# Second graph layer: window sums that begin at the lowest receiver and go to a table in node order

## The chip, the cores and the metric

One core of one Trainium2 chip. The metric is the device time of one launch in microseconds (us). A span is the time from the first to the last instruction of one profiled execution.

## What is computed

A graph of 3125 nodes with 256 features each and 50000 edges, sorted by receiver (`dst`). Two layers follow each other, each with a residual sum and a layer norm:

```
x = layernorm(x + L0(x, edge_attr, src, dst))     # mean over each sender of an MLP times a gate
x = layernorm(x + L1(x, src, dst, w))
```

The change concerns `L1`, attention with four heads of 64 columns:

```
h     = x @ W                                # [nodes, 4 heads, 64]
e     = leaky(a_src[src] + a_dst[dst]) * w   # per edge and head
e_exp = exp(e - max(e))
denom = segment_sum(e_exp, dst)
alpha = e_exp / (denom[dst] + 1e-10)
out   = segment_sum(h[src] * alpha, dst)
```

## The kernel before

The edges are cut into 391 blocks of 128, four blocks to a group (98 groups), two groups to a pair (49 pairs). There are 25 node tiles of 128 rows. All five instruction streams are written out by hand, with semaphores.

**First layer, to about 1610 us.** The matrix engine is busy nearly all the time with the MLP; nothing of it is changed, but for the table that is cleared during it (`HB`, at groups 8 to 10) and two small instructions of constants at the start (`rem_c`).

**Between the layers, to about 1670 us.** The first norm, the products `h` with the score columns, and their table `HT` in DRAM. Ahead of it VectorE works out constants (`win_tile`, `keep`, `in_tile` and a test on the graph, `outside`) while the last additions to the first layer's table land.

**Windows, about 1671 to 2334 us.** GpSimd fetches the sender rows of each block with one indirect DMA (`gather_h_rows`, L1605) into a ring of 12 groups; group g may be fetched when VectorE has weighted group g - 12 (`s_xb`). For each pair q VectorE does, in this order: `weighted_rows(2q)`, `carry_window(2q-2)`, `running_maximum(q+1)`, `edge_scores(q+2)` (it waits for the gathers of pair q+2 and for the product of TensorE that gives the receivers' scores), `weighted_rows(2q+1)`, `carry_window(2q-1)`, `one_hot(q+3)`, `window_rows(q+1)`. Every seventh pair `window_scores` is put in, and once, at q = 3, `last_rows`: eleven instructions (L1153 to L1164), some of 2450 elements per partition, which find for each node the last window that holds it. TensorE sums a group's blocks into one PSUM bank (`window_sums`, L1927): the row of a sum is the receiver modulo 128 (`in_window`). Since the edges are sorted, consecutive groups overlap, and `carry_window` (L1136, L1148) adds to a window the window before, row by row where `keep` says that the row still means the same node, times `drop`, the correction for a raised maximum:

```
dve.scalar_tensor_tensor(hist[:, g % HISTR, 0:BW], hist[:, (g - 1) % HISTR, 0:BW], carried,
                         PS[g % 3][:, 0:BW], ALU.mult, ALU.add).then_inc(s_carry, 1)
```

SP stores each window as 128 rows of the table `HB` (L1485), six of them in flight (`s_hd[g % HISTR]`). ScalarE only takes the exponentials (L2178, L2185, L2187).

**End, from about 2334 us.** VectorE makes `scale` from `last_g` and the factors of the windows (L1192, L1194). When all windows are stored GpSimd fetches, with 25 indirect DMAs (L1671), each node's last window row into `fin`. The tiles go in chunks of 3, 5, 5, 5, 5 and 2. `attention_residual` on VectorE: four small instructions for the denominators (L1298 to L1305), a product of the rows with them into PSUM (`weigh`, L1117), the sum with `xn` (L1321), statistics (L962, L966); `norm_factors` (L994, L996). ScalarE normalises (L2153), SP stores `out` (L1533).

`if_outside` is a branch for graphs on which windows do not suffice. It is not taken here; each engine loads a register and jumps.

Of the kernel before, what the change touches and what calls it, by code (L numbers as in the profile page):

```python
# [6 lines left out]
P = 128  # L7
# [15 lines left out]
def build_program(nc, xT, x, src_cols, dst_cols, src_row, dst_row, eT, w_cols,  # L23
# [50 lines left out]
    ZERO_ROW = NG * P  # L74
    ACC0 = ZERO_ROW + P
    HROWS = ACC0 + TR
# [73 lines left out]
    with ctx:  # L150
# [15 lines left out]
        HB = nc.dram_tensor("HB", [HROWS, BW], f32).ap()  # L166
# [13 lines left out]
        rem_c = sb("rem_c", [P, NB])  # L180
# [22 lines left out]
        zeros = sb("zeros", [P, BW])  # L203
# [36 lines left out]
        rem_ci = sb("rem_ci", [P, NB], i32, sn)  # L240
# [59 lines left out]
        keep = sb("keep", [P, NG], f32, sc)  # L300
# [4 lines left out]
        reached = sb("reached", [P, NT, NG], bf16, sc)  # L305
        in_tile = sb("in_tile", [P, NG, NT], bf16, sc)
        n_f = sb("n_f", [P, NT], f32, sc)
        base_f = sb("base_f", [P, 1], f32, sc)
        passed = sb("passed", [P, NT], f32, sc)
        there = sb("there", [P, NT], f32, sc)  # L310
        row_f = sb("row_f", [P, NT], f32, sc)
        row_i = sb("row_i", [P, NT], i32, sc)
        node = sb("node", [P, NT, HEADS], f32, sc)
        ADC = 14
        picked = sb("picked", [P, ADC, HEADS, NT], f32, sc)
        ad_w = sb("ad_w", [P, NG, HEADS], f32, sc)
# [6 lines left out]
        drop_k = sb("drop_k", [P, NQ], f32, sc)  # L323
        last_g = sb("last_g", [P, NT, NG], bf16, sc)
        factor = sb("factor", [P, NG], f32, sc)
        chosen = sb("chosen", [P, NT, NG], f32, sc)
        scale = sb("scale", [P, NT], f32, sc)
# [19 lines left out]
        hist = sb("hist", [P, HISTR, BW], f32, s2)  # L347
# [10 lines left out]
        trash_u = sb("trash_u", [P, 1], f32, s2)  # L358
# [141 lines left out]
        s_dk = sem("s_dk")  # L500
        s_carry = sem("s_carry")
        s_hd = [sem(f"s_hd{i}") for i in range(HISTR)]
# [20 lines left out]
        VW = C1 + 2 * C2 + 5  # L523
# [22 lines left out]

        assert NG % 2 == 0 and NG % ADC == 0 and ADC % 2 == 0 and HGR > 6 and HGR % 2 == 0
# [67 lines left out]
        def wait_windows_stored(eng):  # L615
            for k in range(HISTR):
                eng.wait_ge(s_hd[k], ring_total(HISTR, k, NG))
# [13 lines left out]
        def _(dve):  # L631
# [116 lines left out]
            for p in range(4, 2 * NT):  # L748
# [23 lines left out]
                if p == 42:  # L772
# [3 lines left out]
                    const(dve.tensor_single_scalar(rem_ci[:, :], dst_c[:, :], P - 1, ALU.bitwise_and))  # L776
# [354 lines left out]
            def carry_window(g):  # L1131
# [6 lines left out]
                if g >= HISTR:  # L1138
                    dve.wait_ge(s_hd[g % HISTR], 16 * (g // HISTR))
# [27 lines left out]
            for q in range(-3, NQ + 1):  # L1167
# [19 lines left out]
                if q == ADC // 4:  # L1187
                    last_rows()
# [1091 lines left out]
```

## Time and profile before

| | |
|---|---|
| median of 3 runs | 2392.39 us (2390.41 to 2396.98) |
| the profiled execution | 2400.63 us, span 2398.6 us |
| mean granted TensorE clock | 0.892 of full speed |
| TensorE matmul, VectorE, ScalarE, GpSimd busy | 1909.3, 1425.6, 1208.7, 1519.2 us |
| first layer | 0 to about 1610 us |
| windows of the second layer | about 1671 to 2334 us |
| end | about 2334 us to 2398.6 us |

The busy shares are means over stages that have different limits, so the windows and the end are read by themselves. In the rows "remote" and "another core or an unknown queue" stand for a releaser that the profile could not name.

### The profile page before, as it was taken

What the parts mean: (1) busy time and instruction counts of PE and PEld (TensorE: products, weight loads), DVE (VectorE), ACT (ScalarE), POOL (GpSimd) and SP (SyncE); (2) the same over time, 40 slices, a digit from 0 to 9 for tenths busy, and PEclk for the clock granted to TensorE, in tenths of its full rate; (3) what the DMA queues carried; (4) which work ended last, traced back from release to release, by engine and by line L of the source; (5) the groups of instructions that cost most, each with busy time, mean ns of one, the idle gap of its engine ahead of it and who ended that gap; (6) DMA issues with size and microseconds to landing.
All of it is one profiled execution on the core that took longest, in us unless ns stands there. A gap on an engine that the chain in (4) does not pass through costs nothing. (4 is left out here: it accounts for less than half of the span.)

```text
span 2398.6 us, 38205 instructions
## 1 busy us (share of the span) xinstructions
PE 1909.3 (80%) x12132; PEld 1633.2 (68%) x12132; DVE 1425.6 (59%) x4037; ACT 1208.7 (50%) x2298; POOL 1519.2 (63%) x1253
## 2 busy tenths in 40 slices
PE   7799999989999999999999999966145555555560
PEld 6688888878888888888888888855033444444440
DVE  6556666556666666666666666646164554554575
ACT  2477677666777777777777777744000000000012
POOL 0417677777777777777777777752745655655623
PEclk9899999999999999999999999988567777667785
DMA  7788877777777777777777877766434544444433
GB/s 245 254 224 185 176 164 165 142 150 171 163 159 161 160 160 161 166 158 159 159 161 167 176 171 173 162 107 194 113 94 118 128 118 128 128 117 129 127 82 110
DMA packets 239708, 370.94 MB, mean 155 GB/s; under 512 B 33256, under 2 KB 172482, under 8 KB 239496
## 3 DMA queue, kind: packets, MB, share of 16 engines
q0 software_dynamic: 104688, 191.38, 40.0%
q1 hardware_dynamic: 134807, 177.00, 25.9%
q8 instruction: 101, 1.65, 0.3%
q14 instruction: 112, 0.91, 0.1%
HBM read 260.28 MB, written 107.97 MB: 154 GB/s over the span
## 5 line engine op out<-in xcount | busy, mean ns | idle before, releaser
L1548 POOL DMA_INDIRECT accA<-ystage,to_a x391 | 642.4, 1643 | 217.0 <-issue 113.3
L1554 POOL DMA_INDIRECT GA<-TA,src_c x391 | 429.7, 1099 | 252.3 <-issue 111.8
L1605 POOL DMA_INDIRECT Hg<-HT,src_c x391 | 375.0, 959 | 255.7 <-DVE xb L1117 147.5
L643 DVE TENSOR_TENSOR h2l<-h2f,h2h 128x512 fp32r<-128x512 f32 (+1 forms) x294 | 203.0, 690 | 314.1 <-ACT h2h L1998 160.1
L1680 PE MATMUL bank<-h1h,W1h 128*128 128x512 f32 x882 | 354.7, 402 | 11.0 <-DVE h1l L643 11.0
L2035 ACT ACTIVATE h1f<-bank 128x512 f32<-128x512 f32 (+1 forms) x392 | 221.0, 590 | 256.9 <-PE bank L1735 196.8
L1682 PE MATMUL bank<-h1h,W1l 128*128 128x512 f32 x882 | 349.1, 396 | 0.0
L1681 PE MATMUL bank<-h1l,W1h 128*128 128x512 f32 x882 | 349.0, 396 | 0.0
L2178 ACT ACTIVATE drop<-neg_m 128x1 f32<-128x1 f32 x49 | 14.4, 295 | 603.6 <-issue 418.3
L1927 PE MATMUL bank<-xb,in_window 128*128 128x260 f32 (+1 forms) x782 | 279.7, 518 | 47.6 <-issue 47.2
L643 DVE TENSOR_TENSOR h1l<-h1f,h1h 128x512 fp32r<-128x512 f32 x294 | 194.3, 688 | 117.8 <-ACT h1h L1998 107.5
L2060 ACT ACTIVATE h2f<-bank,b1c 128x512 f32<-128x512 f32 x294 | 201.9, 687 | 120.4 <-PE bank L1752 95.9
L1927 PEld LDWEIGHTS bank<-xb,in_window 128*128 128x128 f32 (+1 forms) x782 | 194.4, 262 | 96.1 <-issue 59.3
L1916 PE MATMUL bank<-diag,ones 128*128 128x128 f32 x98 | 34.2, 448 | 275.2 <-issue 162.1
L1916 PEld LDWEIGHTS bank<-diag,ones 128*128 128x128 f32 x98 | 23.4, 286 | 293.2 <-issue 172.4
L1680 PE MATMUL bank<-W2h,h2h 128*128 128x256 f32 (+1 forms) x782 | 220.7, 282 | 2.1 <-DVE ystage L809 2.1
L1681 PE MATMUL bank<-W2l,h2h 128*128 128x256 f32 (+1 forms) x782 | 221.0, 283 | 0.0
L1682 PE MATMUL bank<-W2h,h2l 128*128 128x256 f32 (+1 forms) x782 | 221.0, 283 | 0.0
L1680 PEld LDWEIGHTS bank<-h1h,W1h 128*128 128x128 f32 x882 | 167.5, 190 | 42.7 <-DVE h1l L643 11.8
L1682 PEld LDWEIGHTS bank<-h1h,W1l 128*128 128x128 f32 x882 | 166.9, 189 | 39.6
L1681 PEld LDWEIGHTS bank<-h1l,W1h 128*128 128x128 f32 x882 | 167.2, 190 | 37.1
L1998 ACT ACTIVATE h2h<-h2f 128x512 fp32r<-128x512 f32 x294 | 185.4, 631 | 9.4
(252 smaller groups left out, 4490.6 us busy)
## 6 DMA issues: line engine op xcount, KB each, us to landing
ef<-in_eT SPq DMA_DIRECT2D x97, 256.0 KB
bcast_i<-in_src_row SPq DMA_DIRECT2D x97, 256.0 KB
TW<-TB SPq DMA_DIRECT2D x116, 203.0 KB
HB<-hist SPq DMA_DIRECT2D x98, 130.0 KB
rel<-RL SPq DMA_DIRECT2D x97, 128.0 KB
rem<-RD SPq DMA_DIRECT2D x48, 256.0 KB
TB<-stB SPq DMA_DIRECT2D x24, 406.0 KB
accA<-zeros SPq DMA_DIRECT2D x4, 2193.0 KB, 16.4
```

The costliest lines, as they stand in the source:

```text
L643: return dve.tensor_tensor(o, full, hi.bitcast(f32), ALU.subtract)
L1548: return pool.indirect_dma_start(out=table, out_offset=bass.IndirectOffsetOnAxis(ap=rows, axis=0), in_=sums, in_offset=None, compute_op=AL ...
L1554: pool.indirect_dma_start(out=GA[0:n, b % (GAR * BLOCKS_PER_GROUP), :].bitcast(f32), out_offset=None, in_=TA, in_offset=bass.IndirectOffse ...
L1605: pool.indirect_dma_start(out=Hg[0:n, slot, :], out_offset=None, in_=HT, in_offset=bass.IndirectOffsetOnAxis(ap=src_c[0:n, b:b + 1], axis= ...
L1680: pe.matmul(o, lh, rh, start=first, stop=False)
L1681: pe.matmul(o, lh, rl, start=False, stop=False)
L1682: return pe.matmul(o, ll, rh, start=False, stop=last)
L1916: pe.matmul(PTOP[:, 0:P], ones[:, :], diag[:, q % 2, :], start=True, stop=True).then_inc(s_sp, 1)
L1927: last = pe.matmul(PS[g % 3][:, 0:BW], in_window[0:n, j, :], xb[0:n, j, :], start=b == blocks[0], stop=b == blocks[-1])
L1998: return act.activation(o, i, ACT.Copy)
L2035: act.activation(h1f[0:k1(c), c, 0:n], PT[u % 2][0:k1(c), 0:n], ACT.Tanh).then_inc(s_tanh1, 1)
L2060: act.activation(h2f[:, m, 0:n], PL1[u % 2][:, 0:n], ACT.Tanh, bias=b1c[:, m:m + 1]).then_inc(s_tanh2, 1)
```

## The change

1. **Windows begin at the lowest receiver.** `in_window` compares with `rel_c` (receiver less the group's lowest receiver) in place of `rem_c` (receiver modulo 128). A window is then 128 consecutive nodes.
2. **The sum before is carried by a matmul.** VectorE no longer adds in `carry_window`. It builds `to_next`, a unit matrix shifted by the distance between the two windows' first nodes, for even groups times `drop`; TensorE adds `to_next` times the stored window before as a fifth matmul of the group; ScalarE copies the sum out of PSUM (`window_copy`), and a 261st column with the negative maximum of that window.
3. **Stores go to a table in node order.** SP reads the group's lowest receiver into a register and stores the window at that row of `F`. Successive windows overlap there, so each store waits for the one before (one semaphore `s_hd`). `last_rows`, `keep`, `drop_k`, `factor`, `chosen` and `scale` go; a plain load of the 261st column (`row_m`) and one exponential take the place of `scale`.
4. **End.** SP loads `row_m` and the six chunks of `fin` with plain DMAs in place of the 25 gathers. VectorE makes the reciprocal with two instructions; GpSimd multiplies the rows by it in place; VectorE adds and takes the statistics as before.

```diff
-            def carry_window(g):
...
-                dve.scalar_tensor_tensor(hist[:, g % HISTR, 0:BW], hist[:, (g - 1) % HISTR, 0:BW], carried,
-                                         PS[g % 3][:, 0:BW], ALU.mult, ALU.add).then_inc(s_carry, 1)
+            def carry_matrix(g):
...
+                if g >= 3:
+                    dve.wait_ge(s_S, g - 1)
+                o, shifted = to_next[:, g % 2, :], moved[:, g:g + 1]
+                if g % 2:
+                    dve.tensor_scalar(o, iota_p, shifted, None, ALU.is_equal).then_inc(s_next, 1)
+                    return
+                dve.wait_ge(s_drop, g // 2 + 1)
+                dve.tensor_scalar(o, iota_p, shifted, drop[:, g // 2:g // 2 + 1], ALU.is_equal, ALU.mult).then_inc(s_next, 1)
...
-                if q == ADC // 4:
-                    last_rows()
...
 def window_sums(g):   # TensorE
+                if g >= 1:
+                    pe.wait_ge(s_next, g)
+                    pe.wait_ge(s_carry, g)
+                    last = pe.matmul(PS[g % 3][:, 0:BW], to_next[:, g % 2, :], hist[:, (g - 1) % HISTR, 0:BW],
+                                     start=False, stop=True)
...
 # ScalarE
+            def window_copy(g):
+                act.wait_ge(s_S, g + 1)
+                if g >= HISTR:
+                    act.wait_ge(s_hd, 16 * (g - HISTR + 1))
+                copy(hist[:, g % HISTR, 0:BW], PS[g % 3][:, 0:BW])
+                copy(hist[:, g % HISTR, BW:FW], neg_m[:, g // 2 + 1:g // 2 + 2]).then_inc(s_carry, 1)
             for q in range(NQ):
+                if q >= 2:
+                    window_copy(2 * q - 4)
+                    window_copy(2 * q - 3)
...
 # SP
-                        sp.wait_ge(s_carry, g + 1)
-                        sp.dma_start(HB[g * P:(g + 1) * P, :], hist[:, g % HISTR, :]).then_inc(s_hd[g % HISTR], 16)
+                        first = sp.value_load(low_i[0:1, g:g + 1], min_val=0, max_val=N - 1)
+                        sp.wait_ge(s_carry, g + 1)
...
+                            sp.wait_ge(s_hd, 16 * g)
+                        sp.dma_start(F[bass.ds(first, P), :], hist[:, g % HISTR, :]).then_inc(s_hd, 16)
...
+            wait_windows_stored(sp)
+            sp.dma_start(row_m[:, :], F[0:NT * P, BW:FW].rearrange("(t p) d -> p (t d)", p=P),
+                         allow_slow_non_contiguous=True).then_inc(s_rowm, 16)
+            for c in range(NC):
+                tiles = tiles_of_chunk(c)
+                sp.dma_start(fin[:, tiles[0]:tiles[-1] + 1, :],
+                             F[tiles[0] * P:(tiles[-1] + 1) * P, 0:BW].rearrange("(t p) d -> p t d", p=P)).then_inc(s_fin[c], 16)
...
 # GpSimd
-            for t in range(NT):
-                pool.indirect_dma_start(
-                    out=fin[:, t, :], out_offset=None, in_=HB,
...
+            for c in range(NC):
+                pool.wait_ge(s_cinv, NC + c + 1)
+                pool.tensor_tensor(rows, rows, cinv[:, v, :].unsqueeze(3).to_broadcast([P, k, HEADS, HD]), ALU.mult)\
+                    .then_inc(s_att, 1)
...
 # VectorE, end
+            attention_factors(0)
+            for c in range(NC):
+                if c + 1 < NC:
+                    attention_factors(c + 1)
                 if c >= 1:
                     norm_factors(c - 1, NC + c - 1)
+                attention_residual(c)
```

On VectorE, in the middle of the windows, one pair read before (`L1117` is the weighting, `L1079` to `L1101` the scores, `L1148` the carried sum):

```order
L1117 TENSOR_TENSOR xb<-Hg,bank 128x4x256
L1136 TENSOR_TENSOR drop_k<-drop,keep 128x1
L1148 SCALAR_TENSOR_TENSOR hist<-hist,drop_k,bank 128x260
L1108 TENSOR_REDUCE top_g<-bank 128x1
L1112 SCALAR_TENSOR_TENSOR neg_m<-top_g,neg_m 128x1
L1079 TENSOR_TENSOR score<-Hg,bank 128x32
```

and reads now:

```order
L1110 TENSOR_TENSOR xb<-Hg,bank 128x4x256
L1136 TENSOR_SCALAR to_next<-bank,moved,drop 128x128
L1101 TENSOR_REDUCE top_g<-bank 128x1
L1105 SCALAR_TENSOR_TENSOR neg_m<-top_g,neg_m 128x1
L1072 TENSOR_TENSOR score<-Hg,bank 128x32
```

Between the wait for a pair's scores and the weighting behind it nothing is moved.

On TensorE, in the middle of the windows, one pair now reads as follows (`L1898` are the block sums, `L1903` the carried window, `L1878` the receivers' scores, `L1887` the spread of the maxima):

```order
L1887 MATMUL bank<-diag,ones 128x128
L1898 MATMUL bank<-xb,in_window 128x260 x4
L1903 MATMUL bank<-hist,to_next 128x260
L1878 MATMUL bank<-ad_p,hot 128x4 x24
L1898 MATMUL bank<-xb,in_window 128x260 x4
L1903 MATMUL bank<-hist,to_next 128x260
```

The two `L1903` rows are new; the first of them, with its wait for ScalarE, stands ahead of the product for the receivers' scores.

## Rows read from the trace of the kernel before

**Rows 1.** Busy time by stretch (us, then PE, PEld, DVE, ACT, POOL; clock, DMA share, GB/s)

```profile
150.00:1550.00 1400.00, 1369.42 (x8952) 1199.26 (x8951) 893.93 (x2724) 1027.65 (x1855) 1050.68 (x760) 0.99 0.78 166
1900.00:2100.00 200.00, 107.70 (x648) 81.52 (x645) 100.16 (x222) 11.61 (x48) 118.57 (x125) 0.75 0.48 125
```

**Rows 2.** Waits, 1900 to 2100 us (total us, times, longest)

```profile
DVE score L1079 <- remote: 88.3, 13, 9.8
POOL Hg L1605 <- DVE xb L1117: 48.1, 15, 5.0
```

**Rows 3.** Timeline, 1960 to 1991 us (start us, us, instruction, idle before it)

```profile
1960.93 0.75 PE L1907 MATMUL bank<-ad_p,hot 128*128 128x4 bf16 x24
...
1972.79 0.19 DVE L1079 TENSOR_TENSOR score<-Hg,bank 128x32 f32<-128x32 f32 x1 [9.82 <-remote]
...
1978.81 0.82 PE L1907 MATMUL bank<-ad_p,hot 128*128 128x4 bf16 x24
...
1984.18 0.96 POOL L1605 DMA_INDIRECT Hg<-HT,src_c  x1 [0.30 <-issue]
1985.44 0.19 DVE L1079 TENSOR_TENSOR score<-Hg,bank 128x32 f32<-128x32 f32 x1 [6.10 <-remote]
...
1986.54 1.22 DVE L1117 TENSOR_TENSOR xb<-Hg,bank 128x1024 f32<-128x1024 f32 x1
1988.02 0.95 POOL L1605 DMA_INDIRECT Hg<-HT,src_c  x1 [2.89 <-DVE xb L1117]
```

**Rows 4.** Timeline around `last_rows`, VectorE and GpSimd

```profile
1788.21 0.29 DVE L1153 TENSOR_SCALAR n_f<-tile_row,p_f 128x25 f32<-128x25 f32 x1
...
1789.55 2.71 POOL L1605 DMA_INDIRECT Hg<-HT,src_c  x1 [0.30 <-issue]
...
1797.08 1.22 DVE L1117 TENSOR_TENSOR xb<-Hg,bank 128x1024 f32<-128x1024 f32 x1
...
1798.57 0.95 POOL L1605 DMA_INDIRECT Hg<-HT,src_c  x1 [5.05 <-DVE xb L1117]
```

**Rows 5.** Groups by line: VectorE 1750 to 2250 us, TensorE 1900 to 2100 us

```profile
L1148 DVE SCALAR_TENSOR_TENSOR hist<-hist,drop_k,bank 128x260 f32<-128x260 f32 x38 | 18.4, 485 | 8.2 <-DVE drop_k L1136 6.5 <-issue 1.5
...
L1101 DVE TENSOR_SCALAR diag<-ident,top_c 128x128 f32<-128x128 f32 x38 | 12.2, 322 | 1.8 <-issue 0.2 <-DVE top_c L1096 0.2
...
L1136 DVE TENSOR_TENSOR drop_k<-drop,keep 128x1 f32<-128x1 f32 x38 | 5.7, 151 | 0.0
L1927 PE MATMUL bank<-xb,in_window 128*128 128x260 f32 x248 | 90.5, 527 | 11.6 <-issue 11.6
```

**Rows 6.** ScalarE's copies between the layers (ns min/median/max)

```profile
L1998 ACT ACTIVATE hst<-bank x25: 371/390/391, 1633.2 to 1668.2; 128x264 f32<-128x264 f32 x24, 53x264 f32<-53x264 f32 x1
```

**Rows 7.** Timeline of the last pairs of windows and of the first gather behind them

```profile
2306.89 0.16 DVE L1112 SCALAR_TENSOR_TENSOR neg_m<-top_g,neg_m 128x1 f32<-128x1 f32 x1
...
2313.37 0.16 DVE L1112 SCALAR_TENSOR_TENSOR neg_m<-top_g,neg_m 128x1 f32<-128x1 f32 x1
...
2333.38 0.48 DVE L1148 SCALAR_TENSOR_TENSOR hist<-hist,keep,bank 128x260 f32<-128x260 f32 x1 [0.61 <-PE bank L1927]
...
2342.66 0.96 POOL L1671 DMA_INDIRECT fin<-HB,row_i  x1 [43.12 <-issue]
...
2348.21 0.17 DVE L1298 TENSOR_TENSOR cden<-fin,scale 128x12 f32<-128x12 f32 x1 [8.99 <-DMA fin<-HB,row_i]
```

**Rows 8.** Chain that ended last, DMA piece behind the last window

```profile
2333.89 4.46 DMA HB<-hist
```

**Rows 9.** Timeline, SP's loads of single elements (64 of 4 bytes each) and of rows

```profile
319.59 0.60 SPq L1450 DMA_DIRECT2D ablk<-in_a_src x1
```

**Rows 10.** DMA issues of the whole span (KB each, us to landing)

```profile
tab<-accA SPq DMA_DIRECT2D x8, 645.0 KB, 8.0
```

**Rows 11.** Timeline of the end on VectorE

```profile
2366.09 0.42 DVE L962 BATCH_NORM_STATS2 stats<-xn 128x6 f32<-128x256 f32 x1
...
2375.57 0.18 DVE L966 BATCH_NORM_AGGREGATE mv<-stats 128x2 f32<-128x6 f32 x1 [0.52 <-remote]
...
2384.14 0.18 DVE L1300 TENSOR_SCALAR cden<-cden 128x20 f32<-128x20 f32 x1
...
2384.88 1.62 DVE L1117 TENSOR_TENSOR bank<-fin,bank 128x512 f32<-128x512 f32 x3
...
2386.71 1.74 DVE L1321 TENSOR_TENSOR xn<-xn,bank 128x256 f32<-128x256 f32 x5
2388.37 1.72 DVE L962 BATCH_NORM_STATS2 stats<-xn 128x6 f32<-128x256 f32 x5
2390.01 0.43 DVE L966 BATCH_NORM_AGGREGATE mv<-stats 128x2 f32<-128x6 f32 x5
...
2390.52 0.17 DVE L1300 TENSOR_SCALAR cden<-cden 128x8 f32<-128x8 f32 x1
...
2393.40 0.28 DVE L966 BATCH_NORM_AGGREGATE mv<-stats 128x2 f32<-128x6 f32 x2
```

**Rows 12.** Timeline between the layers, VectorE and GpSimd side by side

```profile
1645.46 1.47 DVE L974 TENSOR_TENSOR tab<-tab 128x1290 f32<-128x1290 f32 x1
...
1647.34 0.19 POOL L1613 COPY node<-hst 128x4 f32<-128x4 f32 x1 [0.25 <-ACT hst L1998]
```

**Rows 13.** All GpSimd copies of that line (ns min/median/max)

```profile
L1613 POOL COPY node<-hst x25: 179/187/1162, 1633.8 to 1668.6; 128x4 f32<-128x4 f32 x24, 53x4 f32<-53x4 f32 x1
```

More of the change, by code:

```diff
@@ L322, in build_program @@
         drop = sb("drop", [P, NQ], f32, sc)
[L323 to L327, printed above, removed]
+        row_m = sb("row_m", [P, NT], f32, sc)
+        row_eps = sb("row_eps", [P, NT], f32, sc)
+        log_eps = sb("log_eps", [P, 1], f32, sc)
         Wc = sb("Wc", [P, DK, OUT + 2 * HEADS], f32, sc)
@@ L499, in build_program @@
         s_S = sem("s_S")
-        s_dk = sem("s_dk")
+        s_next = sem("s_next")
         s_carry = sem("s_carry")
-        s_hd = [sem(f"s_hd{i}") for i in range(HISTR)]
+        s_hd = sem("s_hd")
+        s_rowm = sem("s_rowm")
         s_nd = sem("s_nd")
@@ L615, in wait_windows_stored @@
         def wait_windows_stored(eng):
-            for k in range(HISTR):
-                eng.wait_ge(s_hd[k], ring_total(HISTR, k, NG))
+            eng.wait_ge(s_hd, 16 * NG)
         def if_outside(eng):
@@ L1166, in _ @@
+                if g >= 3:
[6 more added lines that the diff above has]
+                dve.tensor_scalar(o, iota_p, shifted, drop[:, g // 2:g // 2 + 1], ALU.is_equal, ALU.mult).then_inc(s_next, 1)
             window_scores(0)
-            for q in range(-3, NQ + 1):
+            for q in range(-3, NQ):
@@ L1285, in _ @@
                                                   ALU.is_equal, ALU.mult))
-                    step(dve.tensor_scalar(to_u[0:n, :], to_f[0:n, 1:2], trash_u[0:n, :], None, ALU.add), ("row", b))
+                    step(dve.tensor_scalar(to_u[0:n, :], to_f[0:n, 1:2], trash[0:n, :], None, ALU.add), ("row", b))
                     dve.wait_ge(s_vg, 64 * NB + 16 * (b + 1))
@@ L1311, in attention_residual @@
-                for j in range(0, k, 2):
-                    m = min(2, k - j)
-                    last = weigh(bank[3 * (c % 2) + j // 2][:, 0:m * OUT].rearrange("p (t d) -> p t d", d=OUT),
-                                 fin[:, t0 + j:t0 + j + m, 0:OUT], factors[:, j:j + m], P, m)
-                last.then_inc(s_att, 1)
+                dve.wait_ge(s_att, c + 1)
+                for t in tiles:
+                    n = rows_of_tile(t)
+                    dve.tensor_tensor(xn[0:n, t, :], xn[0:n, t, :], fin[0:n, t, 0:OUT], ALU.add).then_inc(s_res, 1)
@@ L1322, in attention_residual @@
-                row_stats(tiles, NT)
-            for c in range(NC):
                 attention_residual(c)
@@ L2189, in _ @@
                 last.then_inc(s_ex, 1)
-            for i in range(2):
-                last = act.activation(factor[:, :].rearrange("p (q i) -> p q i", i=2)[:, :, i], neg_m[:, 1:NQ + 1], ACT.Exp,
-                                      bias=neg_m[:, NQ:NQ + 1], scale=-1.0)
-            last.then_inc(s_factor, 1)
+            for g in range(NG - 4, NG):
+                window_copy(g)
             with if_outside(act):
```

140 lines of the change are left out of this document (51 added, 89 removed).

## Prediction

> **What bounds the kernel now.** I first read the busy time by stretch. In the first layer TensorE is busy 1369 of 1400 us, and nothing of the change lies there. In the windows no engine is full: of 200 us TensorE is busy 107.7, VectorE 100.2, GpSimd 118.6, ScalarE 11.6 [rows 1]. So I read the waits next. VectorE loses 88.3 us in 13 waits at the scores (L1079), with no releaser named, and GpSimd loses 48.1 us in 15 waits for VectorE's weighted rows [rows 2]. The timeline of one pair shows how the two hang together. GpSimd's last fetch starts at 1984.18, the score wait ends at 1985.44, the odd group is weighted at 1986.54 for 1.22 us, and only then, at 1988.02, does GpSimd fetch again after 2.89 us of idle time [rows 3]. Eight fetches of 0.96 + 0.30 us are 10.1 us; with the stall of 2.5 to 2.9 a pair takes about 12.6 us. It is a closed loop: ring empty, scores, weighting, ring free. What VectorE does *outside* the 2.5 us between score wait and weighting is hidden in its 6.10 us of waiting [rows 3]. The reader should keep this in mind: the change works nearly only on that outside part.
>
> At the end the fetches of `fin`, VectorE's chunks and the store follow one another. The last window is summed at 2333.38, stored after 4.46 us more, the first denominator starts at 2348.21, and a full chunk takes 6.38 us (2384.14 to 2390.52) [rows 7, 8, 11].
>
> **The change part by part.**
>
> *Steady windows: 0.* Per pair VectorE loses two additions of 0.485 and one product of 0.151, and gains two `to_next` of 128x128, for which the nearest row is `diag`, 0.322 [rows 5]. That is 0.48 us less per pair, in time in which VectorE waits. TensorE gains two products of 260 columns, 2 x 0.527 at the most, on 107.7 us busy in 200 [rows 1, 5]; ScalarE two copies of about 0.39, the price of a copy of 264 columns out of PSUM [rows 6], and two of one column. Cover for both: TensorE ends the receivers' product (L1907, 24 matmuls) at 1961.7 and at 1979.6, while the score waits on it end at 1972.79 and 1985.44, so 11 and 6 us later, and each just as GpSimd has run out of fetches [rows 3]. Stores wait for each other, but two of 4.46 us at the most fit into 12.6 [rows 8]; without that cover six stored windows of slack would be used up first. If TensorE's cover is gone, the second rival holds.
>
> *`last_rows`: -6.6.* It holds VectorE from 1788.21 to 1797.08, 8.87 us, once. The weighting behind it is what GpSimd waits for: it idles 5.05 us, and one fetch beside it takes 2.71 us in place of 0.95 [rows 4]. 5.05 + 1.76 = 6.8, of which I take 6.6, for the part of the stall that every pair has is partly in it. Bounds: 0, if the next gathers absorb it, to 8.9.
>
> *Last pairs: -2.* After the last fetch VectorE sets the pace, 6.48 us per pair (2306.89 to 2313.37) [rows 7]. 0.48 less work and up to 0.2 less waiting in some five pairs give 2 to 4; TensorE with its two more products is nearly as long, so I take 2.
>
> *Last window to first factor: +2.5.* Before it is 2348.21 - 2333.86 = 14.35 us: store 4.46, then GpSimd's start at 2342.66, then the fetch [rows 7, 8]. Now: one more product 0.44 to 0.53, copies 0.39 + 0.25, a store of 4.46 or less, then `row_m`, then the first chunk of `fin`. `row_m` is a load of 3200 single elements of 4 bytes. The one row on such a load issues 64 of them in 0.60 us [rows 9]; scaled to 3200 that is 30 us, and if elements are spread over the queue's engines it is a few: bounds 2 and 30, and I take 8, for the issue row holds a fixed part and is paid once. The first `fin` chunk lies behind it: a load of 645 KB took 8.0 us to land, this one is 400 KB, of which I count 3 beyond `row_m`, since they overlap [rows 10]. 0.5 + 0.6 + 3.9 + 8 + 3 + 0.9 (exponential and reciprocal) = 16.9, against 14.35: +2.5. With the bounds of `row_m` the step is -4 to +25.
> The Trainium skill (DMA: Bandwidth & Descriptors, section Rules for kernel authors) says that a strided last dimension turns into one descriptor per element and names it as a thing to avoid; by that rule this load is nearer to the 30 than to the 2, and the step would be about +24 in place of +2.5. No row here shows a load of this size.
>
> *Chunks of the end: -6.4.* From the first denominator to the end the span now takes 2398.6 - 2348.21 = 50.4 us [rows 7]. VectorE alone then does, per chunk of five tiles, factors 0.45, sums 1.74, statistics 1.72, aggregates 0.43 and norms 0.35: 4.7 us [rows 11]. The product of 1.62 goes to GpSimd as one instruction of 1280 elements in SBUF. No row shows such a product there. GpSimd's copy of 4 columns takes 0.187, as VectorE's small ones take 0.17 [rows 11, 13], so parity, 1.62, is my lower bound; four times that, 6.4, the upper; I take twice, 3.2, nearer to the copy than to the far end.
> With both engines side by side a chunk is VectorE's 4.7 to 4.9. But rows show them in each other's way: GpSimd's copy takes up to 1.162 where VectorE's two-input additions of 1.47 run [rows 12, 13], and a fetch of 0.95 took 2.71 beside `last_rows` [rows 4]. The order on VectorE is factors of chunk c+1, norms of c-1, sums of c. So GpSimd's product of c+1 starts just ahead of norms and sums, which have two SBUF inputs. If the two exclude each other, VectorE stands for the whole 3.2, and then works 4.7 less the factors' end: 7.7 a chunk, above the 6.38 of now. Against this, 10 us go: from 2366.09 to 2375.57 VectorE's statistics and aggregates come one by one with 0.5 to 1.2 us between, 9.7 us for 2.1 of work, while GpSimd still issues fetches [rows 11]; with no fetches of GpSimd left that stretch has no ground. The sum is 5 x 7.7 = 38.5, and 5.5 behind the last aggregate (2393.40 to 2398.6 is 5.2): 44 us, -6.4. Bounds: five chunks of 4.9 and some 7 for the start and the last normalisation, 31.5 (-19); with GpSimd at 6.4 and exclusion, 16 more than my 44 less what the statistics cover, so +6 to +13.
> The Trainium skill (SBUF — State Buffer, section SBUF: two separate sides) says that GpSimd and VectorE share a port under an exclusive lock, which a VectorE operation with two SBUF inputs holds against GpSimd. By that rule the trace agrees: 1.162 in place of 0.187. [...]
>
> *Sum:* -6.6 - 2 + 2.5 - 6.4 = -12.5. The profiled execution took 2400.6 us, 8.2 above the median of 2392.4; 2392.4 - 12.5 = 2380.
>
> **Rivals.**
> 1. *Engines run side by side at the end.* No exclusion, GpSimd at 2 us or so: the end is 31.5, so the sum is about -25 and the time 2367. For it: GpSimd's copies are short in the median [rows 13].  Against: the longest of them.
> 2. *A new loop through ScalarE (slower).* Place: the product L1903 waits for ScalarE's copy of the window before, and the receivers' scores stand behind it on TensorE. TensorE's window sums, 248 of 90.5 us in 200 [rows 5], 5.8 us a pair, become a chain sum, copy, sum. It decides when the score wait ends on the receivers' product and not on the fetches. Price: a carry of 0.44 with 0.64 of copies and signals of 0.3, 1.45 us a pair, times 48 is 70 us: 2450 at full price, about 2415 at half. For it: the score wait has no named releaser, and ScalarE is in order behind exponentials that wait for the same scores. Against: TensorE had finished 6 to 11 us ahead [rows 3].
> 3. *The single-element load or GpSimd's product is slow.* `row_m` at 20 us or more, or products at 6.4: +12 to +22 on my sum, so 2392 to 2402, 2395 in the middle.
> 4. *The change does nothing.* `last_rows` absorbed (0 in place of -6.6) and the end a wash: 2390, no difference.
>
> **How the numbers follow.** The forecast has 0.45, with a range of its own of 2370 to 2390; rival 1 has 0.2, rival 2 0.17, rival 3 0.13, rival 4 0.05. A measurement tells 0.3% (7.2 us) from nothing, so faster is below 2385.2 and slower above 2399.6. Faster: 0.4 of the forecast and 0.2 of the first rival = 0.6. Slower: all of rival 2 and a good third of rival 3, 0.22. The rest, 0.18, is within 0.3%. The range leaves out the far part of rival 1 and most of rival 2: 2362 to 2404.
>
> **What would show it.** Right: the period of a pair in the middle stays at 12.6 us, the wait at the scores stays about 6 us; the stall at 1798 is gone; the chunk on VectorE is 6 to 7.7 us with GpSimd's product at 3 us and longer beside the sum; the first factor is 16 to 18 us behind the last sum. Wrong: L1903 with long idle time behind ScalarE, the score wait ending on TensorE, a `row_m` of tens of us, or GpSimd's product above 6 us with VectorE idle before each sum.

## The result and the profile after

| | before | changed | ratio (95% interval) |
|---|---|---|---|
| the runs shown | 2390.51 us (2386.91 to 2400.23, 20 runs) | 2399.14 us (2391.30 to 2405.38, 20 runs) | 1.0032 (1.0021 to 1.0043) |
| beside it in e13 | 2384.55 us (29 runs) | 2390.90 us (12 runs) | 1.0032 (1.0011 to 1.0053) |
| beside it in e5, on a chip where before takes 2219 us | 2218.60 us (29 runs) | 2212.76 us (12 runs) | 0.9974 (0.9961 to 0.9988) |

Forecast was 2380 us, 0.4% to 0.5% faster. Measured was 0.3% slower, at the edge of what a measurement tells from nothing, and twice the same. On a chip where the kernel before runs 170 us faster the sign turns round. That third row became the key to the case. Launches in a second, slower state are left out of all ratios: one of the kernel before beside e1 to e4 (2462.49 us) and two of e18 (2712.53 and 5719.66 us).

The profiled execution of the changed kernel took 2397.9 us (span 2396.1). It lies near its median, while the one of before lay 10 us above its own. So stages are compared here by their own lengths, and where possible with a second profile of each. From the first fetch of the windows to the last start of a matmul in them:

| stage | before (profile; e16) | changed (profile; e13) |
|---|---|---|
| windows | 661.9; 649.8 us | 682.8; 672.9 us |
| last matmul to first denominator | 15.3; 14.3 us | 10.6; 11.1 us |
| first denominator to the end | 50.4; 49.7 us | 38.6; 38.3 us |

e16 is the kernel before with `last_rows` moved, 2383.61 us in the median. The end gave back 3 to 5 and 12 us; the windows took 21 to 23. Taken crosswise the four profiles give 11 to 33 us for the windows, so the 20 us are good to some 10.

The waits of the windows, 1900 to 2100 us, changed kernel (total us, times, longest), beside [rows 2]:

```profile
DVE score L1072 <- remote: 106.6, 13, 11.1
ACT hist L1974 <- remote: 87.8, 14, 10.0
ACT hist L1974 <- PE bank L1903: 73.4, 12, 6.6
...
POOL Hg L1576 <- DVE xb L1110: 54.4, 15, 5.2
```

VectorE's wait for the scores grew from 88.3 to 106.6 us and GpSimd's stall from 48.1 to 54.4. The busy time in the same stretch (us, PE, PEld, DVE, ACT, POOL) shows the same, 117 fetches where there were 125 [rows 1], one pair's worth or 6% less:

```profile
1900.00:2100.00 200.00, 120.37 (x681) 91.92 (x682) 94.54 (x207) 23.07 (x103) 114.77 (x117) 0.74 0.44 117
```

The granted TensorE clock of the stretch is 0.74 against 0.75 [rows 1] and explains nothing of it (e13 0.76 and e16 0.73, the other way round).

Now a pair in the timeline of the changed kernel, to be read beside [rows 3]:

```profile
1959.39 0.74 PE L1878 MATMUL bank<-ad_p,hot 128*128 128x4 bf16 x24
...
1967.04 0.95 POOL L1576 DMA_INDIRECT Hg<-HT,src_c  x1 [0.30 <-issue]
1970.64 0.19 DVE L1072 TENSOR_TENSOR score<-Hg,bank 128x32 f32<-128x32 f32 x1 [11.12 <-remote]
1970.65 0.39 ACT L1974 ACTIVATE hist<-bank 128x260 f32<-128x260 f32 x1 [7.71 <-remote]
...
1973.06 3.81 PE L1898 MATMUL bank<-xb,in_window 128*128 128x260 f32 x8 [0.38 <-issue]
...
1973.23 1.21 POOL L1576 DMA_INDIRECT Hg<-HT,src_c  x1 [5.24 <-DVE xb L1110]
...
1976.65 0.77 PE L1903 MATMUL bank<-hist,to_next 128*128 128x260 f32 x2
...
1977.26 0.75 PE L1878 MATMUL bank<-ad_p,hot 128*128 128x4 bf16 x24
1977.46 0.39 ACT L1974 ACTIVATE hist<-bank 128x260 f32<-128x260 f32 x1 [6.33 <-PE bank L1903]
```

Three things. L1878's records end at 1960.13, and both VectorE and ScalarE, which wait for two different signals of TensorE, start at 1970.64 and 1970.65. ScalarE's product had ended at 1966.53. Two engines released within 0.01 us, 10 and 4 us behind the work that they wait for, suggest that the release and not the work came late. The whole trace bears this out: in 23 of the 42 middle pairs (scores 4 to 45) the two start within 0.02 us of each other. But not every signal is late. ScalarE starts 0.04 us behind the end of L1903 in 35 of its 67 waits from 1800 to 2250 us (the last row above is one, amid fetches without a break), and about 4 us behind it in most of the others; on the chip of the third row (e5) it is 0.04 in 75 of 75. Second, L1878 now starts behind L1903, 0.6 us after it. L1903 does not wait for ScalarE's copy there: it starts at 1976.65, while the block sums, which last to 1976.87, are still in the records, and so it does in all 46 odd groups of this profile and of e13's. Third, the first fetch behind the stall takes 1.21 us where it took 0.95.

The end on VectorE, GpSimd and ScalarE, one chunk, beside [rows 11]:

```profile
2371.34 2.33 POOL L1643 TENSOR_TENSOR fin<-fin,cinv 128x1280 f32<-128x1280 f32 x1 [4.13 <-DVE cinv L1265]
2371.47 2.21 DVE L984 SCALAR_TENSOR_TENSOR shift<-mv,rstd 128x5 f32<-128x5 f32 x1
2373.61 1.75 DVE L1273 TENSOR_TENSOR xn<-xn,fin 128x256 f32<-128x256 f32 x5
...
2375.29 1.72 DVE L950 BATCH_NORM_STATS2 stats<-xn 128x6 f32<-128x256 f32 x5
2376.93 0.42 DVE L954 BATCH_NORM_AGGREGATE mv<-stats 128x2 f32<-128x6 f32 x5
...
2377.81 2.33 POOL L1643 TENSOR_TENSOR fin<-fin,cinv 128x1280 f32<-128x1280 f32 x1 [4.14 <-DVE cinv L1265]
```

A chunk takes 2377.81 - 2371.34 = 6.47 us. GpSimd's product is 2.33 us. VectorE's five-column `shift`, 0.17 us by itself, lasts 2.21 us beside it and ends where the product ends. Its statistics, one SBUF input each, take 1.72 us as ever.

Between the last window and the first denominator:

```profile
2347.39 0.39 ACT L1974 ACTIVATE hist<-bank 128x260 f32<-128x260 f32 x1 [1.28 <-PE bank L1903]
...
2352.30 0.42 SPq L1494 DMA_DIRECT2D row_m<-F  x1
...
2356.08 0.32 ACT L2227 ACTIVATE row_eps<-row_m,log_eps 128x25 f32<-128x25 f32 x1 [8.22 <-DMA row_m<-F]
...
2357.52 0.17 DVE L1262 SCALAR_TENSOR_TENSOR cden<-row_eps,fin 128x12 f32<-128x12 f32 x1 [10.04 <-DMA fin<-F]
```

The load of 3200 single elements is issued in 0.42 us and its exponential starts 3.4 us behind that.

### The profile page after: what moved, and what is told of

The parts are those of the page before. It is cut to its first block, busy times and chain, and to the rows that moved or that the text cites. A ratio compares the mean times of both kernels' runs of the same rounds, so it can differ in the third digit from the quotient of the medians.

```text
span 2396.1 us, 39366 instructions
## 1 busy us (share of the span) xinstructions
PE 1955.6 (82%) x12326; PEld 1674.4 (70%) x12326; DVE 1394.1 (58%) x3947; ACT 1249.8 (52%) x2493; POOL 1516.4 (63%) x1234
## 4 chain that ended last, share of the span: by engine, by line
PE 57%; another core or an unknown queue 15%; DVE 13%; issue 5%; DMA 4%; ACT 2%; SPq 2%; POOL 1%; DVEq 0%; ACTq 0%; POOLq 0%
PE bank L1651 13%; PE bank L1653 13%; PE bank L1652 13%; PE bank L1706 4%; PE bank L1696 4%; DVE xb L1110 3%; PE bank L1723 3%; DVE in_window L1057 2%; PE bank L1748 2%; PE bank L1747 2%; DMA accA<-ystage,to_a 1%; PE bank L1854 1%; PE bank L1898 1%; DVE hot L1048 1%
## 5 line engine op out<-in xcount | busy, mean ns | idle before, releaser
L1525 POOL DMA_INDIRECT GA<-TA,src_c x391 | 437.7, 1119 | 252.5 <-issue 109.4
L1576 POOL DMA_INDIRECT Hg<-HT,src_c x391 | 381.7, 976 | 271.0 <-DVE xb L1110 163.0
L1974 ACT ACTIVATE hist<-bank 128x260 f32<-128x260 f32 x98 | 38.0, 388 | 530.4 <-remote 257.6
L1898 PE MATMUL bank<-xb,in_window 128*128 128x260 f32 (+1 forms) x782 | 272.2, 508 | 29.9 <-issue 29.3
L1887 PE MATMUL bank<-diag,ones 128*128 128x128 f32 x98 | 35.0, 457 | 258.3 <-DVE diag L1094 184.4
L1898 PEld LDWEIGHTS bank<-xb,in_window 128*128 128x128 f32 (+1 forms) x782 | 187.9, 252 | 75.8 <-issue 41.5
L1072 DVE TENSOR_TENSOR score<-Hg,bank 128x32 f32<-128x32 f32 (+2 forms) x50 | 9.3, 187 | 358.3 <-remote 348.0
L1887 PEld LDWEIGHTS bank<-diag,ones 128*128 128x128 f32 x98 | 23.7, 290 | 276.1 <-DVE diag L1094 198.3
L1651 PEld LDWEIGHTS bank<-h1h,W1h 128*128 128x128 f32 x882 | 167.5, 190 | 45.9 <-DVE h1l L633 10.6
```

Source lines behind the costliest of these rows:

```text
L1525: pool.indirect_dma_start(out=GA[0:n, b % (GAR * BLOCKS_PER_GROUP), :].bitcast(f32), out_offset=None, in_=TA, in_offset=bass.IndirectOffse ...
L1576: pool.indirect_dma_start(out=Hg[0:n, slot, :], out_offset=None, in_=HT, in_offset=bass.IndirectOffsetOnAxis(ap=src_c[0:n, b:b + 1], axis= ...
L1651: pe.matmul(o, lh, rh, start=first, stop=False)
L1898: last = pe.matmul(PS[g % 3][:, 0:BW], in_window[0:n, j, :], xb[0:n, j, :], start=b == blocks[0], stop=g == 0 and b == blocks[-1])
```

## The experiments

The first eight ran on a chip where the kernel before takes 2219 us, as did e17 and e18; e9 to e16 on chips where it takes 2384 us. The kernel before is timed beside each.

**e1 to e4: parts of the window stage, one at a time.** Edits against the changed kernel:

```diff
 # e1, SP
-                        first = sp.value_load(low_i[0:1, g:g + 1], min_val=0, max_val=N - 1)
-                        sp.dma_start(F[bass.ds(first, P), :], hist[:, g % HISTR, :]).then_inc(s_hd, 16)
+                        sp.dma_start(F[31 * g:31 * g + P, :], hist[:, g % HISTR, :]).then_inc(s_hd, 16)
 # e2: window_copy on VectorE (dve.tensor_copy), none on ScalarE
                 if q >= 1:
+                    window_copy(2 * q - 1)      # ahead of running_maximum and edge_scores
...
                     weighted_rows(2 * q + 1)
+                    window_copy(2 * q)
 # e3 (and e15): the order on VectorE
-                one_hot(q + 3)
                 window_rows(q + 1)
+                one_hot(q + 3)
 # e4: window_sums without
-                    last = pe.matmul(PS[g % 3][:, 0:BW], to_next[:, g % 2, :], hist[:, (g - 1) % HISTR, 0:BW],
-                                     start=False, stop=True)
```

> The changed kernel, but SP stores each window at a fixed row (31 times the group) and reads no register for it; the table is then not in node order, so the output is not the reference's. In the changed kernel the windows (first fetch to last window sum) take 683 us, before 663 us. Theory A (the 20 us come from the carried product's chain TensorE, ScalarE, TensorE in the windows): nothing moves, 681 to 685 us. Rival B (SP's reads of low_i and the moving address are the cost): about 665 us and a time near 2380.

> The changed kernel with the window copies on VectorE (one ahead of the wait for the scores, one behind the odd group's weighting) in place of ScalarE. Theory A1 (the copy stands in ScalarE's order ahead of the exponentials and holds them and the next carry): windows 665 to 675 us instead of 683. Rival A2 (TensorE's signals come late whoever waits for them): no gain, 683 us or more, since VectorE then has 1.1 us more per pair of its own and waits for the window's sum ahead of the scores: up to 700 us.

> The changed kernel with VectorE's one_hot (L1048) behind window_rows (L1057) in place of ahead of it. The first fetch behind each stall takes 1.21 us in the changed kernel and 0.95 before: it starts 0.1 us after L1048 there and 0.05 us ahead of it before. Theory C (L1048 keeps GpSimd's fetch waiting when it starts first): every first fetch takes 0.95 again, the windows lose 0.26 us in some 33 pairs, 683 - 9 = 674 us. Rival (the stretch has another ground): 1.21 stays, 683 us.

> The changed kernel without the product L1903: TensorE sums the four blocks alone, ScalarE copies and SP stores as in the change, VectorE still makes to_next. It leaves out the sum over groups of a receiver. Theory A (product and its wait for ScalarE's copy are the cost of the score wait ending 1.55 us in place of 0.26 us behind the last fetch): the score wait ends 0.3 us behind the last fetch again and the windows take 683 - 12 = 671 us (with the fetch stretch of 0.26 a pair left). Rival B (ScalarE's copies, SP's register reads or the stores): still 683 us.

| | time | before beside it | ratio (interval) | windows |
|---|---|---|---|---|
| e1 | 2213.47 us | 2219.19 us | 0.9964 (0.9945 to 0.9982) | 510.1 us |
| e2 | 2214.94 us | 2219.19 us | 0.9974 (0.9955 to 0.9993) | 509.6 us |
| e3 | 2213.87 us | 2219.19 us | 0.9973 (0.9956 to 0.9991) | 508.0 us |
| e4 | 2212.04 us | 2219.19 us | 0.9973 (0.9954 to 0.9992) | 507.3 us |

None of the expectations was met, and none could tell anything apart: the windows take 507 to 510 us here, not 683, whatever is left out. (e1 and e4 do not compute the reference's output: e1 stores at the wrong rows, e4 leaves out the sum over groups.) The waits of e4, 1800 to 2000 us, tell why:

```profile
DVE score L1072 <- DMA Hg<-HT,src_c: 69.3, 18, 4.9
POOL Hg L1576 <- issue: 48.2, 158, 0.3
POOL Hg L1576 <- DVE xb L1110: 0.3, 1, 0.3
```

The score wait ends on the rows that the fetches bring, and GpSimd never runs dry (0.3 us of stall in 200): it issues all the time, 159 fetches in 200 us, 8 x 1.257 = 10.06 us a pair. With that, 838 matmuls in a stretch of 200 us in place of 916 (e4 against e5, 1900 to 2100 us) are worth nothing.

**e5 to e8: the changed kernel itself there, the end, `last_rows`.** e5 is the changed kernel; e8 is e3 and e6 together.

```diff
 # e6, VectorE, end, the loop over chunks
-                if c + 1 < NC:
-                    attention_factors(c + 1)
-                if c >= 1:
-                    norm_factors(c - 1, NC + c - 1)
-                attention_residual(c)
+                dve.wait_ge(s_att, c + 1)
+                attention_residual(c)           # the sums alone
+                if c >= 1:
+                    norm_factors(c - 1, NC + c - 1)
+                if c + 1 < NC:
+                    attention_factors(c + 1)
+                row_stats(tiles_of_chunk(c), NT)
 # e7 (and e16), the kernel before
+            last_rows()
             window_scores(0)
...
-                if q == ADC // 4:
-                    last_rows()
```

> The changed kernel once more, as it is, beside the kernel before on the same chip. In the first four experiments the kernel before took 2219 us and not 2390, and the windows ran at 10.1 us a pair in all four, which is GpSimd's issue alone (8 x 1.257). Theory L (the loss in the windows exists only where the loop ring empty, score wait, weighting is what sets the pair: 12.6 us; where GpSimd never runs dry it is hidden): if the kernel before is near 2219 us again, the changed one is 5 to 12 us faster; if it is near 2390 us, the changed one is 4 to 12 us slower. Rival (the loss is there at either speed): slower by 0.3% both times.

> The changed kernel with another order on VectorE in the end: sums of chunk c, norms of c-1, factors of c+1, then the statistics of c. So GpSimd's product of c+1 runs beside the statistics, which read one SBUF input. Theory X (product and VectorE's operations with two SBUF inputs exclude each other: L984 takes 2.21 us beside the product, 0.17 alone): chunks go from 6.46 to 4.7 or 4.9 us, the end is 6 to 9 us shorter. Rival (VectorE waits for something else there): 6.4 us a chunk.

> The kernel before with last_rows moved ahead of the first window scores, where VectorE waits. It prices that term of the prediction (6.6 us, bounds 0 to 8.9). At 12.6 us a pair (kernel before near 2390 us): 4 to 7 us faster. Where GpSimd sets the pair at 10.1 us: the one stretched fetch only, 1 to 2 us, or if last_rows still empties the ring 5 us.

> The changed kernel with one_hot behind window_rows and with the end's other order: the version that may beat both. Near 2219 us for before: 14 to 20 us faster than before. Near 2390 us: the gain of the end (6 to 9 us) and of the fetches (9 us) on the changed kernel's 2399: 2382 to 2386.

| | time | ratio to before, 2218.60 us (interval) | windows | end |
|---|---|---|---|---|
| e5 | 2212.76 us | 0.9974 (0.9961 to 0.9988) | 507.7 us | 38.3 us |
| e6 | 2207.43 us | 0.9956 (0.9942 to 0.9970) | 507.7 us | 32.9 us |
| e7 | 2217.64 us | 1.0005 (0.9991 to 1.0019) | 512.1 us | 40.5 us |
| e8 | 2209.51 us | 0.9960 (0.9939 to 0.9981) | 507.3 us | 32.9 us |

Theory L held: where GpSimd sets the pair the changed kernel is 5.8 us faster, and its windows are no longer than those of before with `last_rows` moved (507.7 against 512.1). The loss of 20 us is there only where the ring runs dry. e7 was expected 1 to 2 or 5 us faster and shows no difference. e8 is a miss: 14 to 20 us were expected and 9 measured, no more than e6 gives alone.

e6 settles the exclusion. The timeline of its end:

```profile
2183.36 1.67 DVE L950 BATCH_NORM_STATS2 stats<-xn 128x6 f32<-128x256 f32 x5
2183.52 2.33 POOL L1642 TENSOR_TENSOR fin<-fin,cinv 128x1280 f32<-128x1280 f32 x1 [2.56 <-DVE cinv L1265]
...
2185.89 1.77 DVE L1271 TENSOR_TENSOR xn<-xn,fin 128x256 f32<-128x256 f32 x5 [0.52 <-POOL fin L1642]
2187.57 0.18 DVE L982 RECIPROCAL rstd<-std 128x5 f32<-128x5 f32 x1
2187.79 0.17 DVE L984 SCALAR_TENSOR_TENSOR shift<-mv,rstd 128x5 f32<-128x5 f32 x1
```

GpSimd's product is as long as before, 2.33 us, the statistics run beside it undisturbed, and `shift` is back at 0.17. Sums start at 2180.99 and at 2185.89, 4.9 us a chunk. The end lost 5.4 us, and the time 5.3, a little under the 6 to 9 expected.

The end is also where the chips differ once more: that of the kernel before takes 40.5 us here (e7) and 50.4 in its profile. Most of the 10 us are the stretch of [rows 11] in which VectorE's short operations came one by one; it isn't there in e7, although GpSimd fetches there too. Fetches alone are then not its ground.

**e9 to e12: the order on TensorE, and a signal made late.** Where before takes 2384 us, all four on one chip.

```diff
 # e9 (and e12, e14, e17), TensorE: L1878 between the blocks and the carried product of the odd group
-                    window_sums(2 * q + 1)
-                if q + 3 < NQ:
-                    destination_scores(q + 3)
+                    window_sums(2 * q + 1, behind)   # blocks, destination_scores(q + 3), carried product
 # e10 (before), e11 (changed), e12 (e9): the receivers' scores are signalled by SP
-                dve.wait_ge(s_ad, q + 1)
+                dve.wait_ge(s_late, 32 * (q + 1))
...
+                    sp.wait_ge(s_ad, q + 4)
+                    for i in range(2):
+                        if 2 * (q + 3) + i > 0:
+                            sp.wait_ge(s_late, 16 * (2 * (q + 3) + i))
+                        sp.dma_start(late_t[:, :], x[0:1, 0:1]).then_inc(s_late, 16)
```

> The changed kernel with the receivers' product L1878 on TensorE ahead of the odd group's carried product L1903. In the recorded profile at 12.6 us a pair the stretch from one score wait's end to the end of L1878 grew from 6.83 us to 7.4 to 7.7, and the signal behind it came after 5.1 to 6.5 us (5.77 before). Where before takes near 2390 us: theory A3 (what stands ahead of L1878 sets the pair) gives 0.4 us less per pair, 2399 - 16 = 2383; rival A4 (the late signal alone) 2399. Where before takes near 2219 us both say: as the changed kernel there, 2213.

> The kernel before, but VectorE's score wait takes TensorE's signal over two tiny loads of SP, one after the other (some 4 us later than the signal itself); the six store semaphores are three. It imitates the late signal of the recorded profile. Where the windows ran at 10.1 us a pair: L1907's end to the score goes from 3 to about 4.4 us, the loop becomes 6.8 + 4.4 = 11.2 us, the windows 510 + 45 = 555 us and the time 2265. If the signal's lateness is not what sets the pair, it stays at 2219.

> The changed kernel with the same late signal. Theory A3: with the loop in force the changed kernel's 7.4 to 7.7 us ahead of the signal count, 0.6 to 0.9 us more a pair than the kernel before with the late signal: windows 25 to 40 us longer than in e10, less the 10 us that the end and last_rows give back: 15 to 30 us slower than e10. Rival (the changed kernel loses nothing by the loop, but by signals that come later on that chip): 6 to 10 us faster than e10.

> The changed kernel with L1878 ahead of the odd group's L1903 and the late signal. Theory A3: 0.4 us less a pair than e11, so 15 to 20 us faster than e11. Rival: as e11.

| | time | ratio to before, 2383.63 us (interval) | windows |
|---|---|---|---|
| e9 | 2371.02 us | 0.9947 (0.9931 to 0.9964) | 652.8 us |
| e10 | 2485.92 us | 1.0425 (1.0403 to 1.0447) | 756.5 us |
| e11 | 2441.08 us | 1.0236 (1.0219 to 1.0254) | 730.1 us |
| e12 | 2401.42 us | 1.0069 (1.0050 to 1.0088) | 683.5 us |

e9 moves one product of 24 small matmuls ahead of another, takes no work away, and turns 0.3% slower into 0.5% faster. Its windows are 20 to 30 us shorter than the changed kernel's (652.8 against 672.9 and 682.8), and as long as those of the kernel before (661.9 and 649.8), though both carried products are still in it. Its waits, 1900 to 2100 us, against 106.6 us in 13 before the edit:

```profile
DVE score L1072 <- remote: 59.6, 11, 10.8
```

The gain is not a regular loop with one product less in it. Its pairs mostly alternate between 8 to 11 and 14 to 18 us, and L1878's 24 matmuls no longer run in one go:

```profile
1974.05 0.49 PE L1878 MATMUL bank<-ad_p,hot 128*128 128x4 bf16 x14
1975.39 0.16 PE L1878 MATMUL bank<-ad_p,hot 128*128 128x4 bf16 x1 [0.84 <-issue]
1976.80 0.21 PE L1878 MATMUL bank<-ad_p,hot 128*128 128x4 bf16 x2 [1.25 <-issue]
1977.52 0.16 PE L1878 MATMUL bank<-ad_p,hot 128*128 128x4 bf16 x1 [0.52 <-issue]
...
1984.59 0.16 PE L1878 MATMUL bank<-ad_p,hot 128*128 128x4 bf16 x1 [1.25 <-issue]
```

The last matmuls come singly, mostly 0.7 us or a multiple of it apart, with no wait in between that the profile shows, and the score follows at 1987.06. VectorE's short operations in the stretch of [rows 11] are spaced alike (2367.88, 2369.28, 2370.68, 2372.08, 2372.79). So on these chips it is not only signals that come late: at times instructions start late for which the profile shows no wait.

e10 to e12 were meant to make the loop on the other chip. They met a chip where before takes 2384 us, so the delay came on top. It cost 102 us, some 2 us a pair: about half of the 4 us that two loads were expected to take. From the end of the receivers' product to the score it is 8.7 us in the median of the middle pairs, where the profile of before has 5.8. e12 against e11 has the sign of theory A3 and twice the size, 40 us where 15 to 20 were expected. e11 against e10 is a miss: 45 us faster, where 15 to 30 slower was expected. In e10 the score wait ends on SP's tiny loads:

```profile
DVE score L1081 <- DMA late_t<-in_x: 100.3, 11, 12.1
```

They stand in one queue with the other loads and stores of SP, which the two kernels place differently, so the added delay is not the same in both. The pair e10 and e11 settles nothing; e11 and e12 differ by the order on TensorE alone.

**e13 to e16: beside each other on a further chip, where before takes 2384.55 us.** e13 is the changed kernel, e14 is e9, e3 and e6 together, e15 is e3, e16 is e7.

> The changed kernel as it is. Where before takes 2384 to 2391 us: windows 683 us and 0.3% slower than before, so e9's 12.6 us of gain over before are 20 us and more of gain over this (theory A3: the order of L1878 and L1903). Rival: near 2375, then e9's order was worth nothing. Where before takes near 2219: 2213 again.

> The changed kernel with L1878 ahead of the odd group's L1903, one_hot behind window_rows, and the end's other order (factors of the next chunk ahead of the statistics). Where before takes 2384 to 2391: e9's 13 us and the end's 5.5 us, with the fetches' 0.26 us a pair up to 9 more: 18 to 27 us faster than before. Near 2219: as e8, 9 to 10 us faster.

> The changed kernel with one_hot behind window_rows, as e3, where the first fetch lasted 0.95 to 0.98 in either order since GpSimd never ran dry. Where before takes 2384 to 2391: theory C has the first fetch behind each stall at 0.95 in place of 1.21 us and 8 to 12 us less than e13; rival (the loop has slack there, or the later one-hot matrix holds L1878 back by 1.2 us a pair): no gain, or up to 50 us slower.

> The kernel before with last_rows ahead of the first window scores. Where before takes 2384 to 2391: 2 to 7 us faster (my term was 6.6). Near 2219: no difference, as e7.

| | time | ratio to before (interval) | windows | end |
|---|---|---|---|---|
| e13 | 2390.90 us | 1.0032 (1.0011 to 1.0053) | 672.9 us | 38.3 us |
| e14 | 2371.21 us | 0.9951 (0.9932 to 0.9970) | 654.5 us | 32.9 us |
| e15 | 2397.20 us | 1.0044 (1.0024 to 1.0064) | 676.3 us | 38.3 us |
| e16 | 2383.61 us | 0.9992 (0.9977 to 1.0006) | 649.8 us | 49.7 us |

e13 repeats the result, so e9's 0.9947 stands against 1.0032, each against before on its own chip: the order is worth some 20 us. On one chip e14 is 19.7 us faster than e13; less the 5.4 us of the end's order that leaves 14. So 14 to 20 us. e15 refutes theory C as a cause: the fetch behind the stall is 0.95 us again,

```profile
1999.10 0.95 POOL L1576 DMA_INDIRECT Hg<-HT,src_c  x1 [2.73 <-DVE xb L1110]
```

and the time is no better (the intervals of e13 and e15 overlap). Where the 0.26 us a pair went was not seen. e16 prices `last_rows`: -0.9 us, by its interval between -5.5 and +1.4. e14, with that useless third edit, is a miss: 13.3 us faster than before where 18 to 27 had been expected, hardly more than e9 without the end's order.

**e17 and e18.** These met the chip of 2219 us again (before 2220.78 us). e17 is e9 and e6 without e3's edit.

```diff
 # e18, the kernel before, GpSimd, behind the four fetches of a group
+                pool.memset(pause[:, g:g + 1], 0.0)
```

> The changed kernel with L1878 ahead of the odd group's L1903 and the end's other order. Where before takes 2384 to 2391: e9's 12.6 and the end's 5.5 us, 16 to 20 us faster than before, ratio 0.992 to 0.994. Near 2219: 9 to 11 us faster (as e6), ratio 0.995 to 0.996.

> The kernel before with a memset of one element on GpSimd behind the four fetches of each group. Theory S (TensorE's signal is held while GpSimd issues fetches in one go): the score wait ends some us earlier, GpSimd never runs dry and the windows fall from 650 towards 530 us. Rival: nothing moves but the memsets, 0.2 to 0.5 us each, 98 of them: windows 0 to 45 us longer. Near 2219 for before only the second can show.

e17 took 2209.43 us, ratio 0.9946 (0.9927 to 0.9964): 11 us faster than before, as expected. e18 took 2221.93 us, ratio 0.9998 (0.9980 to 1.0017), windows 512.5 us: the short instruction costs nothing there. Theory S was not tested, since the ring does not run dry on that chip.

## Why the prediction was wrong

**Steady windows, 0: this step failed.** It took the 6 and 11 us between the end of L1907's records and the end of the score wait [rows 3] as cover, room in which TensorE may work longer. There was none: what stands ahead of that product counts, although TensorE is idle half the time. The stretch from one score start to the end of the next L1907 is score, diag, block sums, L1907; the change put the carried product of the odd group into it. In the median of the middle pairs it grew from 6.83 us to 7.57 (7.70 in e13), and in e9, with the product behind L1878 again, it is 6.84 and the windows are back at those of before. The carried product of the even group stands behind L1878 and costs nothing that shows. That the rest of the pair, the 6 us to the end of the wait, is the time of a late signal, and that the two together make a loop, is the reading that fits the changed kernel's trace best; e9's irregular pairs and its single matmuls show that it is not the whole of it. The text had both facts, that the wait had no named releaser and that it ended when GpSimd ran dry, and did not let them meet. The second holds for one of its two waits only: that at 1972.79 ended 2.3 us after GpSimd's last fetch.

**Rival 2 had the place, but not the loop.** The receivers' product behind L1903 on TensorE is where the time went, and the condition was as written (it decides when the score wait ends on that product). The chain sum, copy, sum through ScalarE was not there: in the changed kernel's two profiles L1903 of the odd group never waited for a copy. The price of 1.45 us a pair, 70 us (its terms add to 1.38), was too high by a factor of 2.6: a mean pair (scores 10 to 40) went from 12.93 us to 13.49 in the profile, and 12.79 (e16) to 13.35 in e13, both 0.56 us. ScalarE's copies lie in idle time; what counted was the product of 0.6 to 1.07 us ahead of L1878. It got a chance of 0.17 on the ground that TensorE was done 6 to 11 us earlier, the same misreading.

**`last_rows`, -6.6: missed.** It was moved ahead of the windows' steady part in e7 and e16 and gave 1.0005 and 0.9992. The stall of 5.05 us [rows 4] was counted as its own. But stalls of 4.9 to 5 us come without it too ([rows 2] has 5.0 as the longest, far behind `last_rows`). Each follows a pair of 10.6 us without a stall, and the two together take 27.0 us, 1.8 more than two of 12.6: such a stall mostly makes up for one that was missing. The lower bound of 0 fits best.

**Last pairs, -2:** about right. Scores start 5.9 us apart in the changed kernel's last pairs (2321.88 to 2327.77), 6.48 before [rows 7].

**Last window to first denominator, +2.5: sign wrong,** measured -3 to -5. The term mis-sized is `row_m`: 8 us taken, 3.4 measured behind the issue, near the lower bound of 2. The 3 us for the first `fin` chunk were too many as well: it let the first denominator start 1.4 us behind the exponential. The Trainium skill (DMA: Bandwidth & Descriptors, Rules for kernel authors) says that a strided last dimension is lowered to one descriptor per element; the 30 us that the prediction put beside it were scaled from [rows 9], and the trace does not bear them out for this load.

**End, -6.4: right in sign and mechanism,** measured -11.8. Exclusion was forecast as in [rows 12, 13] and is shown by L984 (2.21 us beside the product, 0.17 in e6). The chunk came to 6.47 and not 7.7, mostly because GpSimd's product took 2.33 us and not 3.2. That the 10 us of single steps would go was right, and where they never were the step is worth 2 us (40.5 to 38.3). The ground given for them, GpSimd's fetches, is not enough: e7 has the fetches and no such stretch. So this part of the gain came on a ground that did not hold. The Trainium skill (SBUF — State Buffer, SBUF: two separate sides) says that GpSimd and a VectorE operation with two SBUF inputs lock each other out of a shared port for a whole instruction, whichever starts first. Both orders measured agree: `shift` with two SBUF inputs waits out the product (2.21 us), the statistics with one don't.

**Sum.** Forecast -6.6 - 2 + 2.5 - 6.4 = -12.5. Measured 0 in place of the first, -3 to -5 for the third, -12 for the last, and +21 to +23 in the windows, last pairs among them: +4 to +8, against +8.6 and +6.4 by the medians.

**Left open.** Why the score wait ends 5 to 6 us behind TensorE's product on some chips, and whether the signal, the waiters' own instructions or both come late: two waiters that start together and single matmuls 0.7 us apart fit either. That it has to do with GpSimd's fetches is not shown; e18 ran only where the ring never runs dry, and so did e4, which leaves both carried products out.

## What to carry to other kernels

A gap between the end of a producer's records and the end of the wait on it is slack only if something else is seen to end that wait. Where no releaser is named, test whether what stands ahead of the producer counts, however idle its engine. Put the short product whose result somebody waits for ahead of long ones that nobody waits for: here it cost nothing where before takes 2219 us (e17, 0.9946, with the end's order, against e6's 0.9956) and was worth 14 to 20 us where before takes 2384 us (e9, e14), as much as the end had given back.

When GpSimd and VectorE share a stage, place GpSimd's work beside VectorE's operations with one SBUF input: the same two instruction lists took 6.47 us a chunk in one order and 4.9 in the other.

A difference of a few tenths of a per cent can change its sign with the chip. Before explaining it, look whether the stage that lost is bound by the same thing in each run.

## What was not expected of the hardware

- The kernel before takes 2219 us on one chip and 2384 to 2391 on others. For one instruction list (e7 and e16) the windows start 22 us later and the end takes 9 us more; the rest is in the windows, 512 us against 650. The score wait ends on the fetched rows in the first and has no named releaser in the second.
- Where it is slow, TensorE's L1878 mostly ended 5 to 6.5 us before its waiter started, and in 23 of 42 pairs both waiters of TensorE started within 0.02 us of each other.
- There too, instructions for which the profile shows no wait at times started singly, mostly 0.7 us or a multiple of it apart: 95 gaps of over 0.3 us within L1878's matmuls in e9, none in the changed kernel or on the chip of 2219 us (e5, e7, e17).
- A load of 3200 elements of 4 bytes, each by itself, took 0.42 us to issue and had landed 3.4 us later.
- GpSimd's product of 1280 fp32 columns, both inputs and the result in SBUF, took 2.33 us, and 1.04 us for 512 columns.
- VectorE's L1048, just ahead of a fetch, stretched it from 0.95 to 1.21 us; undoing that gave no time.
